# Modulation folded into two vector operations a tile, and two tiles instead of three modulated by GpSimd

## The reference

```python
h = _layernorm(x) * (1 + ca) + sa
x = x + ga * attention(h)                      # causal, 16 heads
h = _layernorm(x) * (1 + cb) + sb              # the normalise-and-modulate that the change touches
x = x + gb * (routed(h) + relu2(h @ shared_up.T) @ shared_down.T)
```

## Time and profile before

| what | value |
|---|---|
| median of 3 runs | 2964.39 us (2961.06 to 2966.58) |
| the profiled execution's own time | 2973.01 us |
| its span in the profile | 2971.3 us |
| PE busy | 2884.4 us (97%) |
| DVE busy | 2179.5 us (73%) |
| ACT busy | 1341.4 us (45%) |
| POOL busy | 1835.6 us (62%) |

### The profile page before, as it was taken

The page is one execution under the profiler, slowest core; times in us unless marked ns, Lnnn a source line. Parts: engine busy times, 40 slices in busy tenths (PEclk is TensorE's granted clock), DMA queues, the critical chain, the costliest instruction groups (busy, mean ns, idle before and its releaser), DMA issues.

```text
span 2971.3 us, 49852 instructions
## 1 busy us (share of the span) xinstructions
PE 2884.4 (97%) x16480; PEld 2164.5 (73%) x16480; DVE 2179.5 (73%) x5344; ACT 1341.4 (45%) x2436; POOL 1835.6 (62%) x1077
## 2 busy tenths in 40 slices
PE   8999999999999999999999989999999999989996
PEld 5788888766666666666666568888888888878775
DVE  6555555678877887878878678887888878857674
ACT  2222222246666666666666633322332233237664
POOL 1233322258888888888887246667666766655664
PEclk9999999989999999999999999999999999999998
DMA  6555555755556655665556243233323332239996
GB/s 238 210 188 194 197 189 186 222 136 121 117 130 138 137 116 116 136 138 132 117 124 147 86 151 103 82 103 97 114 75 111 100 104 82 75 115 244 234 239 117
DMA packets 281948, 420.53 MB, mean 142 GB/s; under 512 B 48463, under 2 KB 132687, under 8 KB 281742
## 3 DMA queue, kind: packets, MB, share of 16 engines
q1 hardware_dynamic: 259214, 384.22, 45.7%
q0 software_dynamic: 22528, 33.72, 6.0%
HBM read 263.38 MB, written 153.01 MB: 140 GB/s over the span
## 4 chain that ended last, share of the span: by engine, by line
PE 75%; POOL 7%; DMA 5%; issue 5%; DVE 4%; ACT 3%; DVEq 0%; POOLq 0%; SPq 0%; ACTq 0%
PE ffn_ps_m L2198 26%; PE qkv_ps_m L840 12%; PE att_ps_s L1304 7%; PE att_ps_p L1386 7%; PE att_ps_o L1330 7%; PE qkv_ps_m L844 6%; DMA out<-exp_y,exp_tok_add 4%; POOL att_gathered L1105 3%; POOL att_pt L1098 2%; PE att_ps_s L1361 2%; PE att_ps_p L1389 2%; ACT att_pt L1166 1%; PE ffn_ps_t L2217 1%; PE exp_ps_u L1607 1%; PE qkv_ps_t L796 1%
## 5 line engine op out<-in xcount | busy, mean ns | idle before, releaser
L247 DVE CUSTOM_DVE_ANT_0 att_ps_s<-att_ps_s,att_causal 128x512 f32<-128x512 f32 (+1 forms) x992 | 471.0, 505 | 176.7 <-PE att_ps_s L1304 172.7
L1166 ACT ACTIVATE att_pt<-att_ps_p 128x512 f32<-128x512 f32 (+1 forms) x1024 | 524.5, 589 | 145.4 <-PE att_ps_p L1389 110.4
L1304 PE MATMUL att_ps_s<-att_ks,att_qs 96*128 96x512 f32 x1488 | 514.4, 373 | 2.1 <-DVE att_lower L253 0.6
L1386 PE MATMUL att_ps_p<-att_qs,att_ks 98*128 98x512 f32 (+3 forms) x1536 | 499.0, 365 | 8.8 <-ACT att_pt L1166 7.8
L1098 POOL TENSOR_TENSOR att_pt<-att_pt 128x1024 f32<-128x1024 f32 (+2 forms) x153 | 331.0, 2163 | 168.4 <-PE att_ps_o L1330 146.8
L1105 POOL TENSOR_TENSOR att_gathered<-att_gathered,att_pt 128x2048 f32<-128x2048 f32 (+1 forms) x92 | 387.9, 4216 | 7.2
L1919 POOL DMA_INDIRECT slot_info<-ffn_info,ffn_slot x256 | 271.5, 1061 | 182.3 <-DMA slot_info<-ffn_info,ffn_slot 96.6
L253 DVE TENSOR_REDUCE att_lower<-att_ps_s 128x1 f32<-128x512 f32 x496 | 340.6, 687 | 7.4 <-PE att_ps_s L1304 7.4
L1386 PEld LDWEIGHTS att_ps_p<-att_qs,att_ks 98*128 98x128 f32 x1536 | 272.9, 191 | 82.1 <-issue 35.6
L1304 PEld LDWEIGHTS att_ps_s<-att_ks,att_qs 96*128 96x128 f32 x1488 | 276.1, 191 | 74.0 <-DVE att_rowmax L247 27.7
L577 POOL TENSOR_TENSOR qkv_x<-qkv_x,qkv_mod 128x512 f32<-128x512 f32 x60 | 83.4, 1390 | 371.8 <-DVE qkv_x L671 371.8
(11 more groups left out here) (311 smaller groups left out, 6595.5 us busy)
## 6 DMA issues: line engine op xcount, KB each, us to landing
att_qs<-qk_parts SPq DMA_DIRECT2D x96, 512.0 KB, 6.8
att_ks<-qk_parts SPq DMA_DIRECT2D x96, 512.0 KB, 12.7
qk_parts<-qkv_out_hi SPq DMA_DIRECT2D x128, 256.0 KB, 2.2
qk_parts<-qkv_out_lo SPq DMA_DIRECT2D x128, 256.0 KB, 2.4
qkv_x<-x SPq DMA_DIRECT2D x16, 1024.0 KB, 5.6
v_rows<-qkv_out_v SPq DMA_DIRECT2D x64, 256.0 KB, 2.3
att_vs<-v_rows SPq DMA_DIRECT2D x32, 512.0 KB, 16.0
o_parts<-att_o SPq DMA_DIRECT2D x64, 256.0 KB, 7.3
```

The source lines that it names most:

```text
L247: dve.tensor_tensor_reduce(part, part, self.causal[:, UNIT - (c1 - c0):UNIT], scale=1.0, scalar=MASKED, op0=ALU.add, op1=ALU.max, accum_ou ...
L1166: act.activation(tile(c)[:, h, col:UNIT], ps_p[(NPROB * prev.g + n) % NP][:, col:UNIT], ACT.Exp, scale=float(HD) ** -0.5).then_inc(exp_don ...
L1304: pe.matmul(bank("s", cur.g, i)[:, 0:c1 - c0], qs[cur.slot][0:STACK, h, t * P:(t + 1) * P], ks[cur.slot][0:STACK, h, c0:c1], start=True, s ...
L1386: last = pe.matmul(part[:, i * (UNIT - col):(i + 1) * (UNIT - col)], ks[prev.slot][:, h + i, kt * P:(kt + 1) * P], qs[prev.slot][:, h + i, ...
```

## The change

In `attend` and in `norm_first`, the order of the arithmetic becomes ((x - mean) * (1 + cb)) * rstd + sb, in two `scalar_tensor_tensor` operations: subtract and multiply, then multiply and add. Each has two tensor inputs and one column scalar. `norm_first` does this for all four tiles. In `attend`, tiles 0 and 1 (ON_POOL = 2) stay as they were, a `tensor_scalar` on DVE and a multiply and an add on POOL; tiles 2 and 3 take the two new operations on DVE, the first for both tiles and then, behind a wait on DVE's own chain, the second for both. The waits that count POOL's tiles go from 3 to 2 a unit, and turns 2 and 3 wait for their own tile's `norm_done` instead of the unit's last. LINKS is one less. The scatters are unchanged; they stand behind the shorter `modulate`.

```diff
--- before.py
+++ after.py
@@ -164,7 +164,8 @@
         inverse_root(dve, self.dve_own, own, rstd, std, mv[:, :, 1], tmp[:, :, 0])
 
 
-LINKS = 2 * UT + 1 + STAT_LINKS + ROOT_LINKS + 2
+LINKS = 2 * UT + 1 + STAT_LINKS + ROOT_LINKS + 1
+ON_POOL = 2
 
 
 class Bridge:
@@ -1250,21 +1251,16 @@
 
                 late.deviation(dve, 0, 0, bridge.mv, bridge.std, bridge.rstd, bridge.tmp)
                 for t in range(UT):
-                    last = dve.tensor_scalar(late.h2[:, t, :], late.x0[:, t, :], bridge.mv[:, t, 0:1], bridge.rstd[:, t:t + 1],
-                                             ALU.subtract, ALU.mult)
-                last.then_inc(late.dve_own, 1)
-                dve.wait_ge(late.dve_own, CREDIT + LINKS - 1)
-                for t in range(UT):
-                    ht = late.h2[:, t, :]
-                    last = dve.tensor_tensor(ht, ht, bridge.mod[:, 1, :], ALU.mult)
-                    if t < UT - 1:
+                    last = dve.scalar_tensor_tensor(late.h2[:, t, :], late.x0[:, t, :], bridge.mv[:, t, 0:1], bridge.mod[:, 1, :],
+                                                    op0=ALU.subtract, op1=ALU.mult)
+                    if t < ON_POOL:
                         last.then_inc(late.mul_done, 1)
                 last.then_inc(late.dve_own, 1)
                 dve.wait_ge(late.dve_own, CREDIT + LINKS)
                 for t in range(UT):
                     ht = late.h2[:, t, :]
-                    last = dve.tensor_tensor(ht, ht, bridge.mod[:, 2, :], ALU.add)
-                    if t < UT - 1:
+                    last = dve.scalar_tensor_tensor(ht, ht, bridge.rstd[:, t:t + 1], bridge.mod[:, 2, :], op0=ALU.mult, op1=ALU.add)
+                    if t < ON_POOL:
                         last.then_inc(late.h_done, 1)
                 last.then_inc(late.norm_done, UT)
 
@@ -1772,7 +1768,7 @@
 
             def store_h2(b, half):
                 u = b * HALVES + half
-                sp.wait_ge(h_done, CREDIT + PT * (u + 1))
+                sp.wait_ge(h_done, CREDIT + ON_POOL * (u + 1))
                 sp.wait_ge(norm_done, CREDIT + UT * (u + 1))
                 dst = h2_dram[bass.ds(u * UNIT, UNIT), :]
                 sp.dma_start(dst.rearrange("(t p) d -> p t d", p=P), h2[:, :, :]).then_inc(h2_out, 16)
@@ -1871,11 +1867,11 @@
 
             def modulate(b, half):
                 u = b * HALVES + half
-                for t in range(PT):
+                for t in range(ON_POOL):
                     pool.wait_ge(norm_done, CREDIT + UT * u + t + 1)
                     ht = h2[:, t, :]
                     pool.tensor_tensor(ht, ht, mod[:, 1, :], ALU.mult).then_inc(mul_done, 1)
-                    pool.wait_ge(mul_done, CREDIT + PT * u + t + 1)
+                    pool.wait_ge(mul_done, CREDIT + ON_POOL * u + t + 1)
                     pool.tensor_tensor(ht, ht, mod[:, 2, :], ALU.add).then_inc(h_done, 1)
 
             def normalise(u):
@@ -2028,17 +2024,17 @@
                 own += 2 * UT + 1 + STAT_LINKS + ROOT_LINKS
                 dve.wait_ge(tr_done, CREDIT + UT * u)
                 dve.wait_ge(h2_out, CREDIT + 16 * u)
-                for t in range(UT):
-                    last = dve.tensor_scalar(h2[:, t, :], xs[:, t, :], mv[:, t, 0:1], rstd[:, t:t + 1],
-                                             ALU.subtract, ALU.mult)
-                    if t < PT:
-                        last.then_inc(norm_done, 1)
-
+                for t in range(ON_POOL):
+                    dve.tensor_scalar(h2[:, t, :], xs[:, t, :], mv[:, t, 0:1], rstd[:, t:t + 1],
+                                      ALU.subtract, ALU.mult).then_inc(norm_done, 1)
+                for t in range(ON_POOL, UT):
+                    last = dve.scalar_tensor_tensor(h2[:, t, :], xs[:, t, :], mv[:, t, 0:1], mod[:, 1, :],
+                                                    op0=ALU.subtract, op1=ALU.mult)
                 last.then_inc(dve_own, 1)
                 dve.wait_ge(dve_own, own + 1)
-                dve.tensor_tensor(h2[:, PT, :], h2[:, PT, :], mod[:, 1, :], ALU.mult).then_inc(dve_own, 1)
-                dve.wait_ge(dve_own, own + 2)
-                dve.tensor_tensor(h2[:, PT, :], h2[:, PT, :], mod[:, 2, :], ALU.add).then_inc(norm_done, 1)
+                for t in range(ON_POOL, UT):
+                    dve.scalar_tensor_tensor(h2[:, t, :], h2[:, t, :], rstd[:, t:t + 1], mod[:, 2, :],
+                                             op0=ALU.mult, op1=ALU.add).then_inc(norm_done, 1)
 
             def groups(t):
 
@@ -2208,10 +2204,10 @@
                                                  for g in range(NG)]).then_inc(proj_done, 1)
 
             def turn(u, t):
-                if t < PT:
-                    pe.wait_ge(h_done, CREDIT + PT * u + t + 1)
+                if t < ON_POOL:
+                    pe.wait_ge(h_done, CREDIT + ON_POOL * u + t + 1)
                 else:
-                    pe.wait_ge(norm_done, CREDIT + UT * (u + 1))
+                    pe.wait_ge(norm_done, CREDIT + UT * u + t + 1)
                 pe.wait_ge(lo_done, CREDIT + UT * u + t - 1)
                 for k in range(DK):
                     last = pe.transpose(ps_t[t % 2][:, k * P:(k + 1) * P], h2[:, t, k * P:(k + 1) * P], ident[:, :])
```

## The result

The changed kernel took 2982.19 us, the median of 7 runs (2974.35 to 2986.70), against 2964.39 us (2957.91 to 2969.70) before. The ratio is 1.0058, with a 95% interval from 1.0044 to 1.0072: 17 us slower, between 13 and 21. Measured once more later (experiment 8), it came to 1.0045 (1.0029 to 1.0060). The two together say about 1.005, some 15 us. The medians differ by 17.8 us the first time and by 12.0 the second (2976.25 against 2964.26). The forecast was 13.4.

The account below looks back on a forecast made before the run. The tensor engine bounds the feed-forward stage; other engines count only where it waits. Losses of 1.2 (unit 2), 10.9 (units 3 to 14) and 1.3 (unit 1) sum to 13.4 us: 2977.5 us, 8-in-10 range 2962 to 2984.

Parts of the forecast that it names:

- the case itself: Main case, turn 2 waiting in units 1 to 14: 13.4 us slower, range 2972 to 2984; chance 0.72, dearer fused operations included.
- The turns of the two engines: DVE and GpSimd alternate: a held-up two-input DVE operation ends 0.56 us after GpSimd's, a held-up GpSimd operation 1.14 after DVE's.
- The rule of the Trainium skill: The engine second to the shared ports blocks fully: some 20 us more in 14 units, 2998; given no chance of its own.
- The price of the fused operation: A fused operation on DVE beside GpSimd costs as the plain two-input one, 0.684 us; 0.07 more as upper end.
- The slack: Spare time before turn 2 would wait for the first hT_lo: 0.05 us in unit 2, 0.35 in unit 14.
- The term of 0.9 us: Turn 2 comes 0.9 us late in each of the twelve units 3 to 14: 10.9 us.
- Unit 1 and unit 15: Unit 1 loses 1.3 us, its turn 2 coming late; unit 15 loses 0, its 1.19 us wait staying as it is.
- the faster rival: Fused operations run in 0.69 us beside GpSimd without sharing, turn 2 never waits: 2960 to 2962.6 us; chance 0.10.
- the slip: DVE's second addition gets its turn before GpSimd's o_lo subtraction: about 1 us lost together, 2965.4 us; chance 0.12.
- GpSimd's inputs: The loads normalise needs land by 4.0 us after DVE's first operation of a unit; normalise starts at 7.25, sooner than before.
- Unit 0: In norm_first, twelve operations become eight: taken as 0 behind 8 us of cover; 2.7 us gained if the cover were gone.

Follow-up runs that it names:

- experiment 8: The changed kernel measured again beside the kernel before: 2976.25 us, ratio 1.0045.
- experiment 2: The changed kernel, with GpSimd waiting before normalise until the first hT_lo subtraction of the coming unit is done: 2962.10 us, ratio 0.9990 to the kernel before.
- experiment 7: The changed kernel with ON_POOL = 1: GpSimd modulates tile 0 alone, DVE does three tiles in six fused operations; 2989.90 us, ratio 1.0101 to the kernel before.
- experiment 5: The kernel before, with only the hT_lo subtraction of tile 0 moved ahead of output tile 1: 2960.51 us, ratio 0.9999.
- experiment 4: The changed kernel's split alone: two tiles on GpSimd, two on DVE in the old unfused operations, unit 0 as before; 3003.46 us, ratio 1.0131 to the kernel before.
- experiment 3: The changed kernel with ON_POOL = 3: GpSimd modulates three tiles as before, DVE does tile 3 fused; 2963.65 us, ratio 0.9996 to the kernel before.
- experiment 1: The changed kernel with the hT_lo subtraction of tile 0 moved ahead of output tile 1 on DVE: 2964.38 us, ratio 0.9997 to the kernel before.

## Why the prediction was right

- *Its sign and size.* 13.4 us forecast, 14.3 and 15.1 in the stage, about 15 in the timed runs. The range of the case itself, 2972 to 2984, holds the median of 2982.19 and that of experiment 8, 2976.25.
- *The turns of the two engines.* The rules for who ends when were read from the kernel before and held to 0.05 us: add 0 forecast at D+3.86, measured 3.84; the vector part at 7.82, measured 7.78; the first addition at 9.52, measured 9.50; the second at 11.93, measured 11.89; `hT_lo` at 12.53, measured 12.49; turn 2 at 12.67, measured 12.64. The rule of the Trainium skill that was weighed there (page "SBUF — State Buffer", section "Who interferes with whom": whoever comes second fully blocks until the first is through) would have made it 2998, if the whole operation followed the wait. The rows agree that the one that comes second ends behind the first, but not that its whole length follows: the second L2176 ends 0.55 us behind GpSimd's operation, and it takes 0.69 alone (experiment 2).
- *The price of the fused operation.* It was taken as the plain one's while blocked, with 0.07 more as the upper end. Alone it does take 0.06 more, but beside GpSimd that is hidden, and the taken value was right.
- *The slack.* The term of 0.9 us for each of the units 3 to 14 was a little small. From unit 2 to unit 14, D came every 59.20 us before and every 60.21 now, 1.01 more a unit, by the starts at 1813.26 and at the row below. For units 2 to 13 the prediction has 1.2 and eleven times 0.9, 11.2 us; 12.2 was measured. Turn 1 starts at D+11.24 on average in these units now and started at D+11.34 before, which the forecast took as fixed. What was to be seen as PE's wait was also read too high: 0.8 to 1.3 us in each of the units 1 to 14 and some 13 in all was forecast, and it is 0.5 to 1.1 in units 2 to 14, 10.3 together, since 0.17 of each loss shows in no gap.

```profile
2535.84 1.00 DVE L2028 TENSOR_SCALAR ffn_h<-ffn_x,ffn_mv,ffn_rstd 128x512 f32<-128x512 f32 x2
```

- *Unit 1 and unit 15.* Unit 1's wait for GpSimd went from 5.0 to 5.2, as forecast. Its 1.3 us went as forecast in experiment 8's execution (0.3 at turn 0, 1.0 from turn 0 to turn 3). In the first one the mechanism was another, the clock: 1.4 from turn 0 to turn 3, with no wait at turn 2. That this term still came out there is luck. In unit 15 the wait for `hT_lo` went from 1.2 to 0.9 and that for tile 0 from 0.6 to 1.0: together the same, as taken.
- *The rivals.* The fused form takes turns with GpSimd too (1.72 and 1.78 us), so the faster rival fell. The second addition missed its turn in each of the units 1 to 14, so the slip did not come about, though its margin of 0.28 us (0.26 was forecast) is small. In experiment 7 it did get its turn in four units, and took 0.87 us.
- *GpSimd's inputs.* They were forecast to be there by D+4.0. With one tile on GpSimd (experiment 7) it waited for them until D+4.2 to D+6.6 in 13 of 14 units. In the changed kernel it comes to them at D+7.2 and waited for none, so the error had no consequence.
- *Unit 0.* Eight fused operations instead of twelve are through earlier, and nothing came of it: the first transpose still waits for an ACT step of attention, as in the earlier trace rows.

## What to carry to other kernels

Where one engine is full, ask of a change on the others only what it does to the few results that the full engine waits for, and how much slack each has; here the slack was 0.05 to 0.6 us from unit to unit. When the operations of two engines hold one another up, taking work away from one need not free the other: its next job can move up into the gap, as `normalise` did here. And a result that is waited for should stand, in its engine's order, ahead of work that can be held up: that one move gave back the whole loss. In the kernel before, where nothing was lost, it gained nothing and made small waits of its own (experiment 5).

## What the runs showed that was not expected

The order of the turns is stable, but not always. In the kernel before and in the changed one, `hT_lo` of units 2 to 14 comes at the same distance from D within 0.03 us; only PE's turn 1 shifts against D, between D+10.9 and D+11.6. With one tile on GpSimd (experiment 7), units of one and the same program fell into different orders, and `hT_lo` came between D+11.5 and D+13.9. What differed was when a load landed: GpSimd had to wait for it, and where it waited longer DVE got its turns earlier. Why the load landed later in some units stays open. A forecast by such turns holds as long as each engine comes to them at a fixed time; where a DMA decides that time, it needs both outcomes.

PE's clock was the second surprise. In unit 1, PE waits about 5 us for GpSimd. Behind waits of 4.95, 4.96 and 5.22 us (the kernel before, experiments 5 and 8) turn 1 came 7.3 us behind turn 0, and the granted clock over the 9 us from turn 0 was 0.84 or 0.85. Behind waits of 4.96, 4.97, 5.21, 5.23, 5.23 and 5.43 us (experiments 4, 3, 2, 1, the changed kernel and experiment 7) it came 8.6 to 8.8 us behind, at 0.67 to 0.69. So the length of the wait does not decide it, and the changed kernel itself did both; what does decide it is open. Waits of 0.5 to 1.1 us, one in each unit, left the granted clock at 1.00 in the steady part of the changed kernel (the windows row from 1900 to 2500 us), while waits of 2.58, 2.49 and 1.99 us in experiment 4, and one of 2.02 in experiment 7, were each followed by a stretch at 1.2 GHz that cost 1.6 us (0.72 over 6 us each time). Waits of up to 2.42 us in the other units of experiment 4 were not. And the seven executions of the changed kernel went with their mean granted clock: 2974.35 and 2975.48 us at 0.992, the five from 2982.08 to 2986.70 us at 0.986 to 0.989. The clock may thus be most of the spread of the runs; where in the kernel the clock was lower in those five was not seen, as only the first was profiled.
